# Running maximum over keys turned by the vector engine, and layer 1 walked in reverse, in a two-layer cross-attention kernel

## The reference

```
def _cross_attention(q_in, kv_in, wq, bq, wk, bk, wv, bv, wo, bo, bias_k, bias_v):
    qh = (q_in @ wq + bq).reshape(b, q_len, H, K)      # H = 16 heads, K = 128
    kh = (kv_in @ wk + bk).reshape(b, t, H, K)
    vh = (kv_in @ wv + bv).reshape(b, t, H, K)
    kh, vh = each with one bias row appended            # t = 1500 + 1 keys
    weights = softmax(einsum("bqhk,bthk->bhqt", qh, kh) / sqrt(K))
    return einsum("bhqt,bthk->bqhk", weights, vh).reshape(b, q_len, H * K) @ wo + bo

x = x + _cross_attention(layer_norm(x), ctx, ...)       # layer 0
x = x + _cross_attention(layer_norm(x), ctx, ...)       # layer 1, the same ctx
return x + gelu(layer_norm(x) @ w_fc1 + b_fc1) @ w_fc2 + b_fc2
```

## Time and profile before

| | us |
|---|---|
| three timed runs | 1277.78, 1273.21, 1277.22 |
| median | 1277.22 |
| profiled execution, own time | 1276.31 |
| its span in the trace | 1274.5 |
| layer 0: query stage, batches, output stage (start to end in the span) | 12.7 to 64.7, 64.7 to 577, 577 to 634.5 |
| layer 1: query stage, batches, output stage and MLP | 634.5 to 680.5, 680.5 to 1192, 1192 to 1274.5 |

### The profile page before, as it was taken

One profiled execution on the slowest core, in us unless ns is written; L12 is line 12 of the kernel. 1 busy time (PEld: TensorE's weight loads), 2 busy tenths in 40 slices (PEclk: granted clock), 3 DMA queues, 4 the chain that ended last, 5 costly groups with the idle time before them and its releaser, 6 DMA issues.

```text
span 1274.5 us, 26492 instructions
## 1 busy us (share of the span) xinstructions
PE 1245.6 (98%) x8108; PEld 1148.5 (90%) x8108; DVE 771.8 (61%) x1273; ACT 805.6 (63%) x1555; POOL 904.0 (71%) x752
## 2 busy tenths in 40 slices
PE   7999999999999999999999999999999999999998
PEld 6779999999999999998887999999999999999897
DVE  6855656565656565565776656565656565655554
ACT  4745666666666666675575666666666666666755
POOL 4737777777777777678664768686868686866882
PEclk9999999999999999999999999999999999999999
DMA  5401111111111111012341111111111111111131
GB/s 167 129 26 49 38 61 36 60 37 60 37 59 38 59 39 58 31 39 81 117 132 42 38 37 62 37 60 37 60 37 59 39 58 40 56 32 50 50 95 41
DMA packets 32592, 72.75 MB, mean 57 GB/s; under 512 B 4977, under 2 KB 6401, under 8 KB 32545
## 3 DMA queue, kind: packets, MB, share of 16 engines
q1 hardware_dynamic: 32256, 71.65, 18.4%
q10 hardware_dynamic: 288, 0.52, 0.1%
HBM read 71.63 MB, written 0.53 MB: 57 GB/s over the span
## 4 chain that ended last, share of the span: by engine, by line
PE 89%; DVE 4%; issue 2%; ACT 2%; DMA 1%; POOL 1%; DVEq 0%; ACTq 0%; SPq 0%; POOLq 0%
PE psum L731 36%; PE psum L752 13%; PE psum L753 13%; PE psum L754 13%; PE psum L697 4%; PE psum L796 4%; PE psum L763 2%; DVE g_prod L1234 1%; PE psum L738 1%; DMA w_raw<-weights 1%; PE psum L745 1%; PE psum L718 1%; PE psum L647 1%; ACT on L1037 1%; PE psum L663 0%
## 5 line engine op out<-in xcount | busy, mean ns | idle before, releaser
L556 POOL TENSOR_TENSOR pt<-slots,pt 125x512 fp32r<-125x512 f32 (+3 forms) x384 | 450.7, 1178 | 215.5 <-ACT slots L1031 198.5
L731 PE MATMUL psum<-qs,ctx 128*125 128x384 f32 (+1 forms) x2304 | 539.1, 370 | 2.0 <-POOL ctx L501 0.8
L731 PEld LDWEIGHTS psum<-qs,ctx 128*125 128x125 f32 x2304 | 393.9, 186 | 48.1 <-ACT slots L1064 8.3
L752 PE MATMUL psum<-ctx,pt 125*128 125x258 f32 (+1 forms) x1344 | 385.4, 287 | 3.3 <-ACT on L1037 3.2
L753 PE MATMUL psum<-ctx,pt 125*128 125x256 f32 (+1 forms) x1344 | 379.3, 282 | 0.0
L754 PE MATMUL psum<-ctx,pt 125*128 125x258 f32 (+1 forms) x1344 | 378.9, 282 | 0.0
L1322 DVE TENSOR_TENSOR t_max<-psum,t_max 125x512 f32<-125x512 f32 (+1 forms) x320 | 199.7, 624 | 266.9 <-PE psum L731 266.8
L1030 ACT ACTIVATE pt<-slots 125x512 fp32r<-125x512 f32 (+3 forms) x384 | 221.0, 576 | 155.8 <-DVE slots L1310 126.1
L1064 ACT ACTIVATE slots<-psum 125x512 f32<-125x512 f32 (+1 forms) x384 | 207.2, 540 | 168.0 <-DVE t_max L1322 158.9
L752 PEld LDWEIGHTS psum<-ctx,pt 125*128 125x128 f32 (+1 forms) x1344 | 253.5, 189 | 19.3 <-ACT on L1037 12.2
L753 PEld LDWEIGHTS psum<-ctx,pt 125*128 125x128 f32 (+1 forms) x1344 | 254.3, 189 | 5.9
(11 more groups left out here) (101 smaller groups left out, 1015.7 us busy)
## 6 DMA issues: line engine op xcount, KB each, us to landing
nat_stage<-ctx_nat SPq DMA_DIRECT2D x64, 375.0 KB
tr_stage<-ctx_tr SPq DMA_DIRECT2D x64, 375.0 KB, 3.0
w_raw<-weights SPq DMA_DIRECT2D x70, 256.0 KB, 2.7
dk_rest<-dk_rows SPq DMA_DIRECT2D x2, 768.0 KB, 6.1
w_raw<-weights ACTq DMA_DIRECT2D x2, 256.0 KB, 3.4
dk_first<-dk_rows SPq DMA_DIRECT2D x2, 256.0 KB, 5.1
xres<-x_rows SPq DMA_DIRECT2D x4, 112.0 KB, 3.5
out_rows<-xres SPq DMA_DIRECT2D x4, 112.0 KB, 1.9
```

The source lines that it names most:

```text
L556: nc.gpsimd.tensor_tensor(split_weights(h, LO, c), logits(h, c), as_f32(split_weights(h, HI, c)), ALU.subtract).then_inc(pt_lo, 1)
L731: last = mm(scores(h, k), ctx_tr_chunk(half, a, c), qs[h][:, m, half, 0:R], start=(half, a, m) == terms[0], stop=(half, a, m) == terms[-1])
L752: mm(out_bank[:, 0:D + 2], hi, ctx_nat_hi(c), start=(c == 0), stop=False, skip_group_check=True)
```

## The change

1. **Maximum.** `t_max[h]` gets 128 rows, the last 32 of them set once a layer to a very low number before the rows in use are written. At `c == 0` DVE transposes it in blocks of 32x32, all tiles in one instruction, into `MT_BANK`, and reduces each block (`turned_max`): 128 partitions (4 key blocks x 32 queries) by 16 or 12 numbers. PE transposes that once (`max_by_block`), behind the weighted sums of step `c == 0` and not ahead of them; DVE reduces over the four key blocks and repeats the result four times (`group_max`, now on 16 or 12 partitions); PE transposes once more (`max_by_query`, at `c == 1`); DVE spreads each number over a block with a second 32x32 transpose, from PSUM to PSUM (`spread_max`).
2. **Layer 1 in reverse.** `batch_at(l, b)` is `b` in layer 0 and `7 - b` in layer 1. Layer 1 starts with the batch whose context is still in SBUF, so its query stage loads and splits none. The sets of tiles handled early and late at the end of a layer differ in layer 1 (7 tiles late, where it was 3).
3. **Start.** SP loads two of the four groups of x rows first, then `hrow`; ACT loads the other two ahead of its two weight tiles. `hdiff` is computed behind the second group's statistics. ACT waits for the tables later. `value_difference` moves under the PE transposes. `key_bias_product` of heads 0 and 1 goes ahead of the first `query_lo`, that of heads 2 and 3 right behind the second.
4. **Output stage.** ACT converts the weights of the fifth head (`weight_hi` of job `H + 4`) ahead of `head_context` of the third head, not behind it.

The core of the diff:

```diff
-            def max_transposes(h):
-                for j in range(GT[h]):
-                    last = nc.tensor.transpose(MT_BANK[:, j * XT:(j + 1) * XT], t_max[h][:, j * P:(j + 1) * P],
-                                               ident[0:XT, 0:XT])
-                last.then_inc(mt_mm, 1)
-            def spread_max(h):
-                for j in range(GT[h]):
-                    last = nc.tensor.transpose(NB_BANK[0:XT, j * P:(j + 1) * P],
-                                               mx_group[:, j:j + 1].to_broadcast([P, XT]), ident[:])
-                last.then_inc(nb_mm, 1)
+            def max_by_block(h):
+                n = GT[h] * BLOCKS
+                nc.tensor.transpose(MT_BANK[0:n, 0:P], mx_part[:, 0:n], ident[:]).then_inc(mt_mm, 1)
+            def max_by_query(h):
+                n = GT[h] * BLOCKS
+                nc.tensor.transpose(MT_BANK[:, P:P + n], mx_group[0:n], ident[0:n, 0:n]).then_inc(nb_mm, 1)
...
+                def turned_max(b, h):
+                    group = l * GROUPS + b * 2 + h
+                    n, R = GT[h] * BLOCKS, GT[h] * P
+                    dve.wait_ge(max_done, INIT + (group + 1) * (NCT - 1))
+                    dve.wait_ge(max_row_in[h], (l * B + b) * 16 + 16)
+                    dve.wait_ge(ot_out, INIT + group * 2 - 2)
+                    V.transpose(MT_BANK[:, 0:R], t_max[h][:]).then_inc(mt_turned, 1)
+                    dve.wait_ge(mt_turned, INIT + group + 1)
+                    V.tensor_reduce(mx_part[:, 0:n], MT_BANK[:, 0:R].rearrange("p (j t) -> p j t", j=n),
+                                    X, ALU.max).then_inc(mt_reduced, 1)
...
-                    V.tensor_reduce(mx_group[:, 0:n], MT_BANK[:, 0:n * XT].rearrange("p (j t) -> p j t", j=n),
-                                    X, ALU.max).then_inc(max_ready, 1)
+                    V.tensor_reduce(mx_group[0:n].rearrange("p (a q) -> p a q", a=BLOCKS), MT_BANK[0:n, 0:P].rearrange(
+                        "p (a k q) -> p a q k", a=1, q=BLOCK).to_broadcast([n, BLOCKS, BLOCK, BLOCKS]), X, ALU.max).then_inc(max_ready, 1)
+                def spread_max(b, h):
+                    dve.wait_ge(nb_mm, INIT + group + 1)
+                    dve.wait_ge(sub_done, INIT + group * NCT)
+                    V.transpose(NB_BANK[:, 0:R].rearrange("p (j t) -> p j t", j=n), MT_BANK[:, P:P + n].rearrange(
+                        "p (j a) -> p j a", a=1).to_broadcast([P, n, BLOCK])).then_inc(shift_ready, 1)
...
+        def batch_at(l, b):
+            return b if l == 0 else b * -1 + (B - 1)
...
-                        if u == 0:
-                            load_nat(0, l * (B * PIECES) + quad, quad)
-                        if u == 2:
-                            load_tr(0, l * (B * PIECES) + quad, quad)
+                        if l == 0 and u == 0:
+                            load_nat(0, l * KEPT + quad, quad)
+                        if l == 0 and u == 2:
+                            load_tr(0, l * KEPT + quad, quad)
...
+            for g in range(2):
+                sp.dma_start(xres[:, g], x_rows[:, g]).then_inc(x_in[g], 16)
             sp.dma_start(hrow[:], head_rows).then_inc(hrow_in, 16)
-            for g in range(RG):
-                sp.dma_start(xres[:, g], x_rows[:, g]).then_inc(x_in[g], 16)
...
+                        if first_quad and u == 0:
+                            weight_hi(l * JOBS + (H + 4), 0, l * 8 + 5)
```

More of the change, by code:

```diff
@@ L46 @@
 PT_COLS = T // PIECES
+KEPT = (B - 1) * PIECES
 BANK = 512
@@ L1354, in batch_steps @@
                             normalized(b - 1, h, O_BANK)
+                        ended = (b - 1 if h == 0 else b, 1 - h) if (h == 1 or not first) and not (tail and h) else None
+                        if c == 1 and ended:
+                            group_max(*ended)
                         i, ph, pc = lagging(k, SUB_LAG)
@@ L1359, in batch_steps @@
                             chunk_max(b, k, h, c)
-                        if c == 0 and (h == 1 or not first) and not (tail and h == 1):
-                            group_max(b - 1 if h == 0 else b, 1 - h)
+                        if c == 0 and ended:
+                            turned_max(*ended)
+                        if c == 1 and ended:
+                            spread_max(*ended)
                         if k in NAT_STEPS and not first and not tail:
```

182 lines of the change are left out of this document (103 added, 79 removed).

## The result

The changed kernel takes **1264.11 us** (median of four runs, 1263.43 to 1265.37), where the kernel before takes 1277.22: a ratio of 0.991 (95% interval 0.9887 to 0.9933), 13.1 us by the medians and 11.5 by the ratio. Three runs of the kernel before that fell in a slow state (3096.81 us here, 1500.22 and 1342.49 beside the experiments) are left out of the times and ratios. It lies in the predicted range, 5.6 us above the forecast of 1258.5, but the sum behind the forecast was wrong in two large terms that nearly cancel (the steady groups, and the query stage of layer 0). The profiled execution took 1263.43 us, its span 1261.6.

The account below looks back on a forecast made before the run. PE was taken as the bound, busy 1245.6 of 1274.5 us. Terms -15.7 + 1.0 + 2.2 - 3.2 - 2.8 + 0.3 - 0.25 + 0 = -18.45 us gave 1258.5 us beside the median, range 1250 to 1267.

Parts of the forecast that it names:

- the steady groups: Batches apart from each layer's first group: 14 x 0.64 + 16 x 0.42, together -15.7 us, before +1.0 for waits.
- PE passes removed: At group ends: eight small PE passes cost 0.86 us, 0.107 each; six in a 3-tile group cost 0.64.
- PE passes added: Two new small PE passes a group, about 0.11 us each, 0.22 a group; bounds 0.05 and 0.2 a pass.
- rival D: DVE transpose at a quarter of the rate, 2.4 us for 512 columns: +41 us, 1300; chance 0.05.
- Room at step 16: 4-tile groups: room before PE's scores wait for step 14's copy shrinks from 1.7 to 0.4 us; +1.0 for waits.
- rival A: Longer DVE chain delays the copy; scores of step 16 wait 0.3 to 0.5 us per 4-tile group: 1264.5; chance 0.2.
- First group of each layer: Batch 0, no weighted sums to hide DVE's work: +1.1 us a layer, +2.2 in all; from 0 to +4.
- Layer 1's query stage: Casts, subtractions and loads gone, so PE's waits for query_lo and context shrink: -3.2 us; from -1.5 to -4.5.
- C: Layer 1's query stage: reversal saves only where nobody waits, POOL's weight work keeps the 2.6 us wait: 1261; chance 0.08.
- Output stages: PE's waits for the fifth head's weights and masked row go: 1.4 a layer, -2.8 us; layer 1's late tiles +0.3.
- Layer 0's query stage: Later query_lo (1.8 us) balances sooner weight loads behind PE's 6.0 us of waits: 0, bounds -4 and +2.
- rival B's second half: Layer 0's query stage, early products: the three stalls mostly go, 1255; B's chance 0.12, both ways.

Follow-up runs that it names:

- e4_second_pass_128: Changed kernel with the second PE pass of a group over 128 partitions of a zeroed mx_group and 128 identity columns: 1256.07 us, ratio 0.984.
- e1_max_alone: Kernel before with the change of the maximum alone; layer order, start, products and weight conversion as before: 1269.25 us, ratio 0.9954.
- e5_weight_late: Changed kernel with ACT's conversion of the fifth head's weights back behind head_context of the third head: 1267.77 us, ratio 0.9941.

## Why the prediction was right in range and wrong in its sum

- **PE passes removed**, eight for 0.86 us: right. Step `c == 0` fell by 0.41 (0.42 read for its four passes).
- **PE passes added**: the step that failed. I took 0.11 a pass from a row of the same kind, with 0.05 and 0.2 as bounds. The two cost 0.47 together (0.86 less the 0.39 gained). With 128 partitions in the second they cost 0.20, so 0.10 each if they share it alike, and the second as it was built costs 0.37 and its step 2.48 us (2.2 to 2.3 named), above my upper bound, since PE loads its 16 or 12 partitions 0.33 us after the load ahead and not 0.12. All passes in the rows of before had 125 to 128 partitions (80 and 112 outside the batches), and I treated "fewer partitions" as "not dearer". A 4-tile group gained 0.39 and not 0.64, a 3-tile group 0.22 and not 0.42. That makes 9.0; other steps give back 0.8 in hundredths, so it is -8.2 in all, 7.5 less than -15.7. With 128 partitions the loss is gone (`e4_second_pass_128`): a 4-tile group gains 0.66, what the sum had.
- **DVE and rival D**: a transpose takes 0.72 us for 512 columns (0.68 taken, 0.71 from the pages). Right, and D is out.
- **Room at step 16 and rival A** (T is the start of the scores of `c == 0`): T + 6.33 for the subtraction (6.2 predicted), 0.3 us of room (0.4 predicted). No wait slipped through, where I had put +1.0 (PE waited for that copy only in the two first batches, 2.3 us in all); the doubled transpose showed the edge 0.3 us away. A did not happen. That is in part luck: the dear second pass held PE back. With it made cheap (`e4_second_pass_128`) PE's load for step 16 comes 0.26 us sooner in the group and the copy of step 14 ends only 0.05 sooner, so that 0.1 us of room is left; steps 15 and 16 still take 2.12 and 2.13.
- **First group of each layer**: +1.7 and not +1.1. Both waits that I had seen came (1.3 and 1.2 us), but I gave PE back 0.7 for slack that it had only at one of them.
- **Reversed addresses**: missing in the sum. +1.05 us in layer 1's batches.
- **Layer 1's query stage**: -3.55 and -3.2 predicted, 42.5 us, within the 42 to 44 named. Some 1.2 of it is the granted clock, which was 0.97 before and 1.00 after, and not a wait; at equal clock it is -2.3 (44.75 in `e1_max_alone`), so the wait for `query_lo` gave less than I took. C is out all the same: neither it nor POOL stands in front of PE there.
- **Output stages**: -0.85 and not -2.5. The waits for POOL went as predicted and a wait for DVE took their place (1.09 against 1.06 + 0.26), since POOL, now early, shuts DVE out (`e5_weight_late`). I had read POOL's 2.6 us of idling as free time, and it was what DVE lived on.
- **Layer 0's query stage**: 0 taken, -5.1 in the trace, outside -4 to +2 (46.9 us, where 50 to 54 were named). The late `query_lo` came nearly as worked out (17.96 us on the chip, 17.8 by the sum; carried queries at 18.77 where they were at 17.09), and then three stalls of 6.0 us became four short ones of 1.9. That was rival B's second half, priced at 3.5. The rest is clock: behind the third stall of before, two groups of six passes, 1.2 us each elsewhere in the stage, took 4.1, at a granted clock of 0.58.

```profile
39.60:43.70 4.10, 4.09 (x13) 3.71 (x14) 3.10 (x6) 2.56 (x5) 3.88 (x3) 0.58 0.33 77
```

- **The sum itself**: beside the median it should read 1258.8 (1277.22 - 18.45), not 1258.5; nothing hangs on it. The room at step 16 was rounded up too: 9.38 - 0.64 - 8.45 is 0.3, as measured, not 0.4.
- **Start**: +0.1 and not -0.25. The x rows landed sooner, but `hrow` landed 0.6 us after DVE was ready for it, and the norm waited behind `hdiff`.

In sum: the batches' steady groups gave 6.5 us less than forecast, first groups and reversed addresses 2.3, the output stages 1.7, start and MLP 0.5; against that stand 5.1 us of a stage put at zero and 0.35 of the other. The difference is the 5.5 us by which the profiled time missed. The range held by that cancelling, which is luck.

## What to carry to other kernels

Before making an operand smaller, look whether any row of the trace has that shape: here a transpose over 16 partitions cost more than three times one over 128, and padding it with zeros won 7.1 us in the batches, where the whole rewrite of the maximum had won 4.8. An idle stretch of GpSimd is not free to fill where VectorE runs two-input SBUF instructions beside it. And read small terms from distances between repeated steps, which repeat to 0.01 us, where executions scatter by 2 to 3.

## What the runs showed of the hardware

- A PE pass with an operand of 12, 16 or 64 partitions between passes of 125 or more is loaded 0.33 us after the load ahead and not 0.12, and the load behind comes late too (0.16 after one of 16 partitions, 0.31 after a pair of 12): some 0.25 us more for one pass. With 96 or 128 partitions there is no such gap.
- A two-input DVE subtraction in SBUF takes 1.09 us where POOL is idle at its start, 1.22 where it meets the last 0.3 us of a POOL instruction, and 1.90 to 2.48 where it stands behind more of them; it ends 0.95 us after the one that it waited for. Hundredths decide who goes first, and with it a microsecond of the stage.
- Waits of PE can cost a second time: the granted clock was 0.58 and 0.66 in the windows behind two of 2.1 and 1.9 us, and 0.73 behind three of 0.3 to 0.6, at 1.2 to 1.6 us each. Behind the same waits in another layer or another execution (1.9 us in layer 0 of the same trace, 0.3 to 0.6 us in the changed kernel) it stayed at 1.00.
